# Two attention blocks on one core: scaled fp16 parts in place of f32r parts, and the row sum scaled on ScalarE

## The chip, the cores and the metric

One of the eight cores of a Trainium2 chip runs the kernel. The metric is the device time of one execution in microseconds. Before the change the median of 3 runs is 421.03 us (420.3 to 421.5).

## The reference

`x` is 4 images of 256 channels by 1024 positions, float32. Two blocks follow each other:

```python
# block 0, for each image
h = group_norm(x)                                  # 32 groups of 8 channels
q, k, v = wq@h + bq, wk@h + bk, wv@h + bv
w = softmax(q.T @ k / 16)                          # 1024 x 1024
x = x + wo @ (v @ w.T) + bo
# block 1, on the result
att_c = softmax(rowmax(x@x.T) - x@x.T)             # 256 x 256, over channels
fb, fc, fd = wb@x + bb, wc@x + bc, wd@x + bd       # 32, 32 and 256 channels
att_s = softmax(fb.T @ fc)                         # 1024 x 1024
out = (beta * att_c@x + x) + (alpha * fd@att_s.T + x)
```

## The kernel before, in words

**Precision by parts.** A product of two float32 operands is made of three matmuls: high by high, high by low and low by high (`product`, lines 872 to 875, where L873, L874 and L875 are the three in order). In block 1 and in all attention sums the parts are fp16. In block 0 the normalised input (`xn_h`, `xn_l`), the folded weights A = wq^T wk (`a_w`) and B = (wo wv)^T (`b_w`) and the projected rows (`g_h`, `g_l`) are float32r parts. The scores of block 1 come from `fb_parts` and `fc_parts`, also float32r, which hold all three products stacked in 96 rows, so that one matmul (L997) does the work of three.

**Steps.** For each image b of block 0: statistics (`bn`, `MEAN`, `spread`, `VAR`, `gvar`, `rstd`, `st1`), normalisation (`xn`, `xnh`, `xnl`; in halves `x0n`, `x0h`, `x0l` for image 0), two projections `G.b.c` (12 matmuls of 512 columns), two `V.b.u` (24 of 256 columns), eight score tiles `S0.b.j` of 128 rows (12 matmuls of 512 columns) and two sums `O0.b.c`. For each image of block 1: `FBC`, `FD`, the channel attention (`ATT`, `AT`, `ET`), eight score tiles `S2.b.j` (2 matmuls of 512 columns) and two sums `O2.b.c`.

**A score tile's way** (64 of them): TensorE fills a PSUM slot (three slots, `SLOTS`, each of two banks, handed round among all steps in PE order); VectorE takes the negative row maximum (`max`, L690) and, for S2 only, scales it (L694); ScalarE takes the exponential with the row sum (`exp`, L422, which gives an ACTIVATE and an ACTIVATION_READ_ACCUMULATOR); VectorE scales the row sum (L702) and takes its reciprocal (L704), both being step `r`; ScalarE makes the high fp16 piece (`a`, L431) and VectorE the low one (`b`, L550); a DMA transpose on SP's queue brings both to `land`; the sum `O` reads them. `exps` and `pieces` have two buffers each, so the exponential of tile n waits for the pieces of tile n-2.

**Order.** Five lists written out by hand (`PE_ORDER`, `ACT_ORDER`, `DVE_ORDER`, `POOL_ORDER`, `SP_ORDER`, lines 25 to 88) give the order of steps on every engine; each engine does them strictly in order and waits on semaphores. `Ox3` means three of a sum's steps (each 6 matmuls).

**The start.** SP's queue loads x of image 0, the group-norm vectors, wo, wv, wd and small vectors, then x of images 1 and 2; ScalarE's queue loads wk, bq and wq. TensorE multiplies the weights (`BG` for the bias, `A`, `B`, and `W` for the rest) while VectorE makes the statistics; `SV` finds bounds of the weights from which `lS` (`fixed_scales`, lines 611 to 642) makes powers of two that scale the fp16 parts. VectorE's list starts with

```python
    bn.0 gb spread.0 gvar.0 st1.0 x0n.0.0 x0n.0.1 bn.1 x0n.1.0 x0l.0.1 lA x0l.0.0 lB x0n.1.1 spread.1 hb gvar.1 cb
    lG.0.0 lS max0.0.0 st1.1 bnd.0 r0.0.0 xn.1.0 max0.0.1 max0.0.2 r0.0.1 b0.0.0 b0.0.1 max0.0.3 r0.0.2 bn.2 lV.0.1
```

`G.0.0` needs the low and high parts of A and of the first half of the input; `S0.0.0` needs `lG.0.0` and the parts of both halves.

## Time and profile before

| what | value |
|---|---|
| runs | 420.3, 421.03, 421.5 us |
| the profiled execution's own time | 419.87 us |
| its span, first to last instruction | 418.1 us |
| TensorE matmuls | 399.9 us busy, 96% of the span |
| TensorE weight loads (beside the matmuls) | 253.9 us, 61% |
| VectorE | 307.5 us, 74% |
| ScalarE | 240.4 us, 57% |
| GpSimd | 47.5 us, 11% |
| granted TensorE clock, mean | 0.998 of full speed |

Engines in the rows: PE is TensorE's matmul, PEld its weight load, DVE is VectorE, ACT ScalarE, POOL GpSimd, SP SyncE; a q behind a name is that engine's queue. L12 is line 12 of the kernel. The end of a matmul is modelled and matmuls are pipelined, so one matmul's duration (380 to 410 ns) is longer than the distance from one start to the next; what a matmul costs is read from starts. `a<-b` is output and inputs, `x` a count.

### The profile page before, as it was taken

The numbers are of one execution on the slowest core, as the hardware profiler recorded it, in microseconds if no ns is written. First come the engines' busy times: TensorE is split into PE (matmuls) and PEld (weight loads), VectorE is DVE, ScalarE is ACT, GpSimd is POOL, SyncE is SP. The second block draws the span as 40 slices with busy tenths as digits, with TensorE's granted clock in tenths as the row PEclk, the third lists the DMA queues.
The fourth block names the chain that finished last, engine by engine and source line by source line (L and its number), as shares of the span: only waits on it lengthen the run. The fifth ranks groups of instructions, "written<-read, shape, count | busy, mean of one in ns | idle before, by whom it ended". The sixth has DMA issues, their size and how long they took to land.

```text
span 418.1 us, 5612 instructions
## 1 busy us (share of the span) xinstructions
PE 399.9 (96%) x2012; PEld 253.9 (61%) x2012; DVE 307.5 (74%) x564; ACT 240.4 (57%) x314; POOL 47.5 (11%) x47
## 2 busy tenths in 40 slices
...
GB/s 229 261 45 19 119 114 96 89 68 186 17 100 122 78 88 118 101 120 157 103 88 114 51 102 125 151 102 50 163 140 57 134 88 152 104 195 124 167 192 51
DMA packets 155739, 47.89 MB, mean 115 GB/s; under 512 B 152320, under 2 KB 153664, under 8 KB 155712
## 3 DMA queue, kind: packets, MB, share of 16 engines
...
q14 instruction: 11, 0.09, 0.1%
...
## 4 chain that ended last, share of the span: by engine, by line
PE 86%; DVE 7%; SPq 2%; issue 2%; DMA 1%; ACT 1%; POOL 0%; DVEq 0%; ACTq 0%
PE sum_ps L873 14%; PE sum_ps L875 14%; PE sum_ps L874 14%; PE score_ps L873 12%; PE score_ps L875 12%; PE score_ps L874 12%; PE score_ps L997 4%; PE score_ps L1018 3%; DVE pieces L550 1%; DMA x<-in_x_dram 1%; DVE bn_raw L726 1%; PE score_ps L1027 1%; DVE x L852 1%; SPq L292 1%; SPq L278 1%
## 5 line engine op out<-in xcount | busy, mean ns | idle before, releaser
L550 DVE SCALAR_TENSOR_TENSOR pieces<-exps,recip,pieces 128x1024 f16<-128x1024 f32 x64 | 88.6, 1388 | 19.9 <-ACT pieces L431 19.5
L431 ACT ACTIVATE pieces<-exps,recip 128x1024 f16<-128x1024 f32 x64 | 72.9, 1143 | 37.6 <-DVE recip L704 27.6
L690 DVE TENSOR_REDUCE negmax<-score_ps 128x1 f32<-128x1024 f32 x64 | 77.4, 1215 | 10.8 <-PE score_ps L997 5.3
L422 ACT ACTIVATE exps<-score_ps,negmax 128x1024 f32<-128x1024 f32 x32 | 35.6, 1112 | 38.1 <-DVE negmax L690 31.7
L873 PE MATMUL score_ps<-xn_h,g_h 128*128 128x512 f32 x128 | 52.8, 412 | 1.1 <-DVE g_l L547 1.1
L422 ACT ACTIVATE exps<-score_ps,negmax_s,scales 128x1024 f32<-128x1024 f32 x32 | 38.4, 1201 | 24.2 <-DVE negmax_s L694 13.8
L875 PE MATMUL score_ps<-xn_h,g_l 128*128 128x512 f32 x128 | 50.1, 391 | 0.0
L874 PE MATMUL score_ps<-xn_l,g_h 128*128 128x512 f32 x128 | 49.9, 390 | 0.0
L873 PE MATMUL sum_ps<-land,fd_h 128*128 128x512 f16 x128 | 48.8, 381 | 0.0
L873 PE MATMUL sum_ps<-land,v_h 128*128 128x512 f16 x128 | 48.7, 381 | 0.0
L874 PE MATMUL sum_ps<-land,fd_h 128*128 128x512 f16 x128 | 48.5, 379 | 0.0
L875 PE MATMUL sum_ps<-land,fd_l 128*128 128x512 f16 x128 | 48.5, 379 | 0.0
L874 PE MATMUL sum_ps<-land,v_h 128*128 128x512 f16 x128 | 48.5, 379 | 0.0
L875 PE MATMUL sum_ps<-land,v_l 128*128 128x512 f16 x128 | 48.5, 379 | 0.0
L378 POOL TENSOR_TENSOR x_parts<-x,x_parts 128x1024 f16<-128x1024 f32 x7 | 15.9, 2272 | 138.3 <-ACT x_parts L395 138.3
L364 POOL TENSOR_TENSOR xn_l<-xn,xn_h 128x1024 fp32r<-128x1024 f32 x6 | 15.5, 2600 | 131.9 <-ACT xn_h L408 87.0
L873 PEld LDWEIGHTS score_ps<-xn_h,g_h 128*128 128x128 f32 x128 | 24.1, 188 | 7.2 <-DVE g_l L547 1.2
L875 PEld LDWEIGHTS score_ps<-xn_h,g_l 128*128 128x128 f32 x128 | 24.0, 188 | 5.3
L874 PEld LDWEIGHTS score_ps<-xn_l,g_h 128*128 128x128 f32 x128 | 24.1, 188 | 4.9
L997 PE MATMUL score_ps<-fc_parts,fb_parts 96*128 96x512 f32 x64 | 24.5, 465 | 0.0
L859 DVE SCALAR_TENSOR_TENSOR x<-sum_ps,scales,x 128x512 f32<-128x512 f32 x16 | 11.3, 745 | 17.2 <-PE sum_ps L875 17.2
L873 PEld LDWEIGHTS sum_ps<-land,fd_h 128*128 128x128 f16 x128 | 12.5, 98 | 17.7 <-issue 5.2
...
## 6 DMA issues: line engine op xcount, KB each, us to landing
...
land<-pieces SPq DMA_TRANSPOSE x64, 3.7
...
```

The lines of the kernel that those rows point to most:

```text
L364: pool.tensor_tensor(xn_l[:, m, :], xn[:, m, :], xn_h[:, m, :].bitcast(f32), ALU.subtract)\
L378: pool.tensor_tensor(x1_parts[b % 2][:, c, :, 1, :], xs[b][:, :, cols(c, QC)], x1_parts[b % 2][:, c, :, 0, :], ALU.subtract).then_inc(x1_s ...
L422: act.activation(exps[:, n % 2, :], score_ps[s][:, :], ACT.Exp, bias=bias, scale=scale, accum_out=rowsum[:, at]).then_inc(score_done[s], 1)
L431: act.activation(pieces[:, n % 2, 0, :], exps[:, n % 2, :], ACT.Copy, scale=recip[:, n % RING:n % RING + 1]).then_inc(high_piece, 1)
L550: return dve.scalar_tensor_tensor(dst, src, scale, high_part, ALU.mult, ALU.subtract)
L690: last = dve.tensor_reduce(negmax[:, at], ps[:, :], AX.X, ALU.max, negate=True)
L859: dve.scalar_tensor_tensor(part, sum_ps[m][:, :], of_batch(b, OUT_UNIT), part, ALU.mult, ALU.add).then_inc(sum_done[m], 1)
L873: pe.matmul(dst, lhs[0], rhs[0], start=start, stop=False)
L874: pe.matmul(dst, lhs[0], rhs[1], start=False, stop=False)
L875: return pe.matmul(dst, lhs[1], rhs[0], start=False, stop=stop)
L997: last = pe.matmul(ps[:, cols(n, QC)], fb_parts[0:3 * C8, cols(j)], fc_parts[0:3 * C8, cols(n, QC)], start=True, stop=True)
L1018: last = pe.matmul(ps[:, cols(m, QC)].rearrange("p (a k q) -> p a k q", a=2, k=CH), xt[:, c, m, 0, u, :], xt[:, c, :, :, u, :].rearrange(" ...
```

## The change

- The f32r tensors of block 0 and of block 1's scores become fp16, which needs scales: bounds on h (`HX`, `hs`), on the rows of wq (`wkA`, `wqA`, `rb`) and on A's product (`TG`, `gs`) give powers of two for h, A and g; B is copied from PSUM (`cB`), bounded in `SV` by two more matmuls, and cut into parts once `lS` is done (`hB`, `lB`). The group-norm bound (`hb`) goes to the head of VectorE's list.
- Every exponential now has a scale read from memory and a scaled maximum: the scores of block 0 need it too, so `max` has its second instruction for all 64 tiles.
- The row sum is scaled on ScalarE, behind the exponential and after a wait for it, in place of VectorE.
- gn_w, gn_b and bq are loaded from GpSimd's queue, ahead of its constants; wo and wv move from SP's queue to ScalarE's, behind wk and wq.
- All five orders are new. In VectorE's, `bn.1` and `x0n.1.0` move behind the low parts that `G.0.0` needs.

The core of the diff:

```diff
...
+PIECES = {"S0": 2.0 ** 15, "S2": 2.0 ** 11}
 PIECE = 2.0 ** 15
...
 PE_ORDER = """
-    BG MEAN.0 WO VAR.0 A B W MEAN.1 G.0.0 VAR.1 SV S0.0.0 S0.0.1 S0.0.2 S0.0.3 V.0.1 G.0.1 V.0.0 S0.0.4 S0.0.5
-    S0.0.6 S0.0.7 O0.0.0x3 MX.0 O0.0.0x2 G.1.0 O0.0.0x3 S0.1.0 S0.1.1 S0.1.2 O0.0.1x2 MEAN.2 S0.1.3 O0.0.1x4 VAR.2
...
+    BG MEAN.0 WO HX VAR.0 A TG W B G.0.0 MEAN.1 SV S0.0.0 S0.0.1 S0.0.2 S0.0.3 G.0.1 V.0.0 VAR.1 S0.0.4 S0.0.5 V.0.1
+    S0.0.6 S0.0.7 O0.0.0x6 MEAN.2 G.1.0 MX.0 O0.0.0x1 VAR.2 O0.0.0x1 S0.1.0 S0.1.1 S0.1.2 S0.1.3 O0.0.1x3 MX.1
+    O0.0.1x5 FBC.0.0 FD.0.0 V.1.0 FBC.0.1 V.1.1 O0.1.0x1 S2.0.0 ATT.0 S2.0.1 O0.1.0x1 AT.0 O0.1.0x2 S2.0.2 O0.1.0x1
...
 ACT_ORDER = """
...
+    hWO wkA wqA x0h.0.0 x0h.0.1 x0h.1.0 hA hW1 x0h.1.1 cB hG.0.0 hB exp0.0.0 exp0.0.1 a0.0.0 a0.0.1 exp0.0.2 hG.0.1
+    exp0.0.3 hV.0.0 a0.0.2 a0.0.3 hW2 exp0.0.4 exp0.0.5 a0.0.4 xnh.1.0 hV.0.1 xnh.1.1 a0.0.5 exp0.0.6 exp0.0.7
...
 DVE_ORDER = """
...
+    hb bn.0 gb spread.0 hs gvar.0 rb st1.0 x0n.0.0 x0n.0.1 gs hw x0l.0.0 lA x0l.0.1 bn.1 x0n.1.0 cb x0n.1.1 aB
+    spread.1 lG.0.0 lS max0.0.0 max0.0.1 r0.0.0 max0.0.2 r0.0.1 b0.0.0 lB b0.0.1 max0.0.3 lG.0.1 r0.0.2 r0.0.3
+    gvar.1 lV.0.0 st1.1 max0.0.4 b0.0.2 b0.0.3 max0.0.5 r0.0.4 bn.2 r0.0.5 lW xn.1.0 xn.1.1 b0.0.4 max0.0.7 lV.0.1
...
-        a_w = [sb(f"a_w_{p}", [P, CH, C], f32r) for p in "hl"]
-        b_w = [sb(f"b_w_{p}", [P, CH, C], f32r) for p in "hl"]
+        a_w = [sb(f"a_w_{p}", [P, CH, C], f16) for p in "hl"]
+        b_w = [sb(f"b_w_{p}", [P, CH, C], f16) for p in "hl"]
...
-        xn_h, xn_l = sb("xn_h", [P, CH, N], f32r), sb("xn_l", [P, CH, N], f32r)
-        g_h, g_l = sb("g_h", [P, CH, QC], f32r), sb("g_l", [P, CH, QC], f32r)
+        xn_h, xn_l = sb("xn_h", [P, CH, N], f16), sb("xn_l", [P, CH, N], f16)
+        g_h, g_l = sb("g_h", [P, CH, QC], f16), sb("g_l", [P, CH, QC], f16)
...
-        fb_parts, fc_parts = sb("fb_parts", [P, N], f32r), sb("fc_parts", [P, N], f32r)
...
+        fb_parts, fc_parts = sb("fb_parts", [P, N], f16), sb("fc_parts", [P, N], f16)
+        abs_w, abs_bbc = sb("abs_w", [P, 2 * CH, C], f32r), sb("abs_bbc", [P, CH, 3 * C8], f32r)
+        h_wide, ones_r = sb("h_wide", [P, CH, P], f32r), sb("ones_r", [P, P], f32r)
...
-            load_v(GN_W, gn_w, gn_loaded)
-            load_v(GN_B, gn_b, gn_loaded)
-            load_w(wo_sb, wo, wo_loaded)
-            load_w(wv_sb, wv, wv_loaded)
...
+            for n, v, loaded in ((GN_W, gn_w, gn_loaded), (GN_B, gn_b, gn_loaded), (BQ, bq, bq_loaded)):
+                with nc.allow_non_contiguous_dma(reason="vectors of 256 words"):
+                    pool.dma_start(vecs[:, n, :], v.rearrange("(m p) -> p m", p=P)).then_inc(loaded, 16)
...
-            act.dma_start(wk_sb, wk.rearrange("(m p) c -> p m c", p=P)).then_inc(wk_loaded, 16)
...
-            act.dma_start(wq_sb, wq.rearrange("(m p) c -> p m c", p=P)).then_inc(wq_loaded, 16)
+            for dst, src, loaded in ((wk_sb, wk, wk_loaded), (wq_sb, wq, wq_loaded), (wo_sb, wo, wo_loaded),
+                                     (wv_sb, wv, wv_loaded)):
+                act.dma_start(dst, src.rearrange("(m p) c -> p m c", p=P)).then_inc(loaded, 16)
...
-                if kind(use) == "S0":
-                    bias, scale = negmax[:, at], 1.0
-                else:
-                    bias, scale = negmax_s[:, at], of_batch(numbers(use)[1][0], SCORE_UNIT)
-                act.activation(exps[:, n % 2, :], score_ps[s][:, :], ACT.Exp, bias=bias, scale=scale,
+                act.activation(exps[:, n % 2, :], score_ps[s][:, :], ACT.Exp, bias=negmax_s[:, at], scale=unit_of(use),
                                accum_out=rowsum[:, at]).then_inc(score_done[s], 1)
+                act.wait_ge(score_done[s], SCORE[use][1] + 1)
+                act.activation(scaled[:, at], rowsum[:, at], ACT.Copy, scale=1.0 / PIECES[kind(use)])\
+                    .then_inc(scaled_made, 1)
...
+                if name == "wkA":
+                    act.wait_ge(wk_loaded, 16)
+                    act.activation(abs_w[:, 0:CH, :], wk_sb, ACT.Abs).then_inc(wk_abs, 1)
+                elif name == "wqA":
+                    act.wait_ge(wq_loaded, 16)
+                    for m in range(CH):
+                        last = act.activation(abs_w[:, CH + m, :], wq_sb[:, m, :], ACT.Abs,
+                                              accum_out=vecs[:, WQ_SUM, m:m + 1])
+                    last.then_inc(wq_abs, 1)
+                elif name == "hA":
                     s, ps = full("A")
...
+                    act.wait_ge(a_scale_made, 1)
+                    act.activation(a_w[0][:, :, :], rows_of(ps[:, 0:QC]), ACT.Copy,
+                                   scale=block0[:, A_SCALE:A_SCALE + 1]).then_inc(score_staged[s], 1)
+                elif name == "cB":
+                    s, ps = full("B")
+                    high(b_full[:, :, :], rows_of(ps[:, 0:QC])).then_inc(score_done[s], 1)
...
                 elif name == "hB":
-                    s, ps = full("B")
-                    high(b_w[0][:, :, :], rows_of(ps[:, 0:QC])).then_inc(score_staged[s], 1)
+                    act.wait_ge(fixed_made, 1)
+                    act.activation(b_w[0][:, :, :], b_full[:, :, :], ACT.Copy,
+                                   scale=fixed[:, B_SCALE:B_SCALE + 1]).then_inc(b_high, 1)
...
+            def h_scale():
+                s, ps = wait_full("HX")
+                dve.tensor_reduce(of0(H_MAX), ps[:, 0:P], AX.X, ALU.max).then_inc(score_done[s], 1)
+                dve.wait_ge(score_done[s], SCORE["HX"][1] + 1)
+                link(dve.tensor_scalar(of0(H_MAX), of0(H_MAX), 1.01, LEAST, ALU.mult, ALU.max))
+                power_of_two(H_MAX)
+                dve.tensor_scalar(of0(U_SCALE), of0(H_INVERSE), 2.0 ** 3, None, ALU.mult)
+                link(dve.tensor_scalar(of0(U_UNIT), of0(H_POWER), 2.0 ** -4, None, ALU.mult))
+                dve.tensor_scalar(vecs[:, U_W, :], vecs[:, GN_W, :], of0(U_SCALE), None, ALU.mult)
+                dve.tensor_scalar(vecs[:, U_B, :], vecs[:, GN_B, :], of0(U_SCALE), None, ALU.mult).then_inc(affine0_made, 1)
+                dve.wait_ge(affine0_made, 1)
+            def r_bound():
+                dve.wait_ge(bq_loaded, 16)
+                dve.wait_ge(wq_abs, 1)
+                link(magnitude(vecs[:, BQ_BOUND, :], vecs[:, BQ, :]))
+                link(dve.scalar_tensor_tensor(vecs[:, R_BOUND, :], vecs[:, WQ_SUM, :], of0(H_MAX), vecs[:, BQ_BOUND, :],
+                                              ALU.mult, ALU.add))
+                for m in range(CH):
+                    last = dve.tensor_scalar(h_wide[:, m, :], ones[:, :], vecs[:, R_BOUND, m:m + 1], None, ALU.mult)
+                last.then_inc(r_bound_made, 1)
+            def g_scales():
+                s, ps = wait_full("TG")
+                dve.tensor_reduce(of0(T_MAX), ps[:, 0:C], AX.X, ALU.max).then_inc(score_done[s], 1)
+                dve.wait_ge(score_done[s], SCORE["TG"][1] + 1)
+                link(dve.tensor_scalar(of0(T_MAX), of0(T_MAX), 1.01, LEAST, ALU.mult, ALU.max))
+                power_of_two(T_MAX)
+                _, used, _ = SCORE["BG"]
+                dve.wait_ge(score_done[SCORE["BG"][0]], used + 1)
+                dve.tensor_scalar(vecs[:, G_BIAS, :], vecs[:, K_BIAS, :], of0(T_INVERSE), 2.0 ** 13, ALU.mult, ALU.mult)
+                dve.tensor_scalar(of0(A_SCALE), of0(T_INVERSE), 2.0 ** 13, of0(U_UNIT), ALU.mult, ALU.mult)
+                dve.tensor_scalar(of0(SCORE_0), of0(T_POWER), 2.0 ** -14 * float(C) ** -0.5, of0(U_UNIT),
+                                  ALU.mult, ALU.mult).then_inc(a_scale_made, 1)
+                dve.wait_ge(a_scale_made, 1)
...
-                last = dve.tensor_reduce(negmax[:, at], ps[:, :], AX.X, ALU.max, negate=True)
-                if kind(use) == "S2":
-                    b = numbers(use)[1][0]
-                    link(last)
-                    last = dve.tensor_scalar(negmax_s[:, at], negmax[:, at], of_batch(b, SCORE_UNIT), None, ALU.mult)
-                last.then_inc(score_staged[s], 1)
+                link(dve.tensor_reduce(negmax[:, at], ps[:, :], AX.X, ALU.max, negate=True))
+                dve.tensor_scalar(negmax_s[:, at], negmax[:, at], unit_of(use), None, ALU.mult)\
+                    .then_inc(score_staged[s], 1)
...
-                s, used, _ = SCORE[use]
-                dve.wait_ge(score_done[s], used + 1)
-                dve.tensor_scalar(scaled[:, at], rowsum[:, at], 1.0 / PIECE, None, ALU.mult).then_inc(scaled_made, 1)
...
+                for m in range(CH):
+                    last = pe.matmul(ps[:, QC + C:QC + 2 * C], ones_r[:, :], abs_w[:, m, :], start=(m == 0),
+                                     stop=(m == CH - 1))
...
-                    done("B")
+                    pe.wait_ge(b_made, 1)
...
+                elif name == "HX":
+                    pe.wait_ge(h_diag_made, 1)
+                    s, ps = enter(step)
+                    pe.matmul(ps[:, 0:P], ones[:, :], x_diag[:, :], start=True, stop=True).then_inc(score_full[s], 1)
+                elif name == "TG":
+                    pe.wait_ge(wk_abs, 1)
+                    pe.wait_ge(r_bound_made, 1)
+                    s, ps = enter(step)
+                    for m in range(CH):
+                        last = pe.matmul(ps[:, 0:C], h_wide[:, m, :], abs_w[:, m, :], start=(m == 0), stop=(m == CH - 1))
+                    last.then_inc(score_full[s], 1)
...
```

## Rows read from the trace of the kernel before

**Rows 1.** The page, busy time of the engines: us (share of the span) xinstructions.
```profile
PE 399.9 (96%) x2012; PEld 253.9 (61%) x2012; DVE 307.5 (74%) x564; ACT 240.4 (57%) x314; POOL 47.5 (11%) x47
```
**Rows 2.** Busy time by stretch: us, engines' busy (xinstructions), PEclk, DMA share, GB/s.
```profile
28.60:50.00 21.40, 21.39 (x116) 18.52 (x117) 19.46 (x57) 12.97 (x18) 0.00 (x0) 1.00 0.22 50
110.00:160.00 50.00, 50.00 (x269) 32.49 (x268) 42.84 (x86) 34.40 (x45) 8.88 (x4) 1.00 0.37 85
360.00:390.00 30.00, 30.00 (x167) 16.79 (x166) 27.10 (x49) 21.57 (x32) 2.67 (x5) 1.00 0.68 159
```
**Rows 3.** TensorE's waits from 28.6 to 413.5 us: us, times, longest.
```profile
PE score_ps L873 <- DVE g_l L547: 1.1, 1, 1.1
PE score_ps L873 <- DVE fc_parts L547: 0.6, 1, 0.6
PE sum_ps L873 <- DVE x L859: 0.4, 1, 0.4
```
**Rows 4.** Timeline of TensorE: start, us (modelled), line, out<-in, shape.
```profile
113.38 0.28 PE L873 MATMUL score_ps<-d_w_h,x_parts 128*128 128x256 f16 x1
...
116.01 0.38 PE L873 MATMUL sum_ps<-land,v_h 128*128 128x512 f16 x1
...
189.53 0.38 PE L875 MATMUL score_ps<-x_parts,bbc_w_l 128*96 128x512 f16 x1
...
192.55 0.28 PE L873 MATMUL score_ps<-b_w_h,xn_h 128*128 128x256 f32 x1
...
195.42 0.63 PE L997 MATMUL score_ps<-fc_parts,fb_parts 96*128 96x512 f32 x2
...
196.99 0.38 PE L875 MATMUL sum_ps<-land,fd_l 128*128 128x512 f16 x1
...
197.68 0.39 PE L873 MATMUL sum_ps<-land,fd_h 128*128 128x512 f16 x1
...
198.77 0.38 PE L875 MATMUL sum_ps<-land,fd_l 128*128 128x512 f16 x1
...
201.74 0.39 PE L873 MATMUL sum_ps<-land,fd_h 128*128 128x512 f16 x1
...
389.25 0.38 PE L873 MATMUL sum_ps<-land,fd_h 128*128 128x512 f16 x1
...
399.39 0.38 PE L875 MATMUL sum_ps<-land,fd_l 128*128 128x512 f16 x1
```
**Rows 5.** Groups by line and shape: busy us, mean ns of one, idle before and releaser.
```profile
L422 ACT ACTIVATE exps<-score_ps,negmax_s,scales 128x1024 f32<-128x1024 f32 x32 | 38.4, 1201 | 24.2 <-DVE negmax_s L694 13.8 <-DVE pieces L550 10.2
L422 ACT ACTIVATE exps<-score_ps,negmax 128x1024 f32<-128x1024 f32 x32 | 35.6, 1112 | 38.1 <-DVE negmax L690 31.7 <-DVE pieces L550 6.4
L422 ACT ACTIVATION_READ_ACCUMULATOR exps<-score_ps,negmax 128x1 f32 x32 | 6.1, 192 | 0.0
L450 ACT ACTIVATE fc_parts<-sum_ps 128x192 fp32r<-128x192 f32 x1 | 0.3, 322 | 0.0
L702 DVE TENSOR_SCALAR scaled<-rowsum 128x1 f32<-128x1 f32 x64 | 9.4, 147 | 11.7 <-ACT exps L422 11.1
L694 DVE TENSOR_SCALAR negmax_s<-negmax,scales 128x1 f32<-128x1 f32 x32 | 6.9, 214 | 1.1
```
**Rows 6.** The start: VectorE's and TensorE's timeline, TensorE's wait, loads and GpSimd's issues.
```profile
16.95 2.47 DVE L726 BATCH_NORM_STATS2 bn_raw<-x 128x6 f32<-128x512 f32 x4 [2.04 <-DMA x<-in_x_dram]
...
28.61 0.47 PE L873 MATMUL score_ps<-xn_h,g_h 128*128 128x512 f32 x1 [1.06 <-DVE g_l L547]
...
PE score_ps L893 <- DMA vecs<-in_L_conv_bq_dram: 7.8, 1, 7.8
...
vecs<-in_L_conv_gn_b_dram SPq DMA_DIRECT2D x1, 1.0 KB, 7.9
...
L383 POOL DMA_DIRECT2D out_dram<-x x16 | 8.8, 553 | 75.9 <-DVE x L859 75.8
```

More of the change, by code:

```diff
@@ L95, in kind @@
+TWICE = {"A", "G", "V", "S0", "S2", "FBC", "FD", "ATT", "ET"}
 def kind(step):
@@ L260, in of_batch, with unit_of @@
             return scales[0:rows, b, n:n + count]
+        def unit_of(use):
+            if kind(use) == "S0":
+                return block0[:, SCORE_0:SCORE_0 + 1]
+            return of_batch(numbers(use)[1][0], SCORE_UNIT)
         def turn_of(use):
@@ L591, in magnitude, with powers @@
                 return dve.scalar_tensor_tensor(dst, src, -1.0, src, ALU.mult, ALU.max)
+            def powers(bound, up, down):
+                dve.tensor_scalar(up.bitcast(u32), bound.bitcast(u32), EXPONENT, None, ALU.bitwise_and)
+                return dve.tensor_scalar(down.bitcast(u32), bound.bitcast(u32), EXPONENT, EXPONENT,
+                                         ALU.bitwise_xor, ALU.bitwise_and)
             def h_bound():
@@ L598, in h_bound, with of0, power_of_two @@
                                               ALU.mult, ALU.add))
+                link(dve.tensor_reduce(x_bound[:, 0, 0:1], vecs[:, H_BOUND, :], AX.X, ALU.max))
                 dve.wait_ge(consts_made, 8)
-                dve.tensor_scalar(ones_r, ones[:, :], 1.0, None, ALU.mult)
+                dve.tensor_scalar(x_diag[:, :], ident[:, :], x_bound[:, 0, 0:1], None, ALU.mult).then_inc(h_diag_made, 1)
+            def of0(n):
+                return block0[:, n:n + 1]
+            def power_of_two(n):
+                link(powers(of0(n), of0(n + 1), of0(n + 2)))
@@ L601, in h_bound, with h_wide_bound @@
+            def h_wide_bound():
+                s, used, _ = SCORE["TG"]
+                dve.wait_ge(score_full[s], used + 1)
+                dve.tensor_scalar(ones_r[:, :], ones[:, :], 1.0, None, ALU.mult)
                 for m in range(CH):
@@ L603, in h_bound @@
                 last.then_inc(h_bound_made, 1)
-            def powers(bound, up, down):
-                dve.tensor_scalar(up.bitcast(u32), bound.bitcast(u32), EXPONENT, None, ALU.bitwise_and)
-                return dve.tensor_scalar(down.bitcast(u32), bound.bitcast(u32), EXPONENT, EXPONENT,
-                                         ALU.bitwise_xor, ALU.bitwise_and)
             def fixed_scales():
@@ L642, in fixed_scales @@
+                dve.tensor_scalar(of(by_unit, 3), of(ones, 0), 2.0 ** -7, None, ALU.mult).then_inc(fixed_made, 1)
                 dve.wait_ge(fixed_made, 1)
@@ L772, in _ @@
                     dve.wait_ge(xn0_high, CH * c + m + 1)
-                    low(xn_l[:, m, half], xn[:, m, half], xn_h[:, m, half].bitcast(f32)).then_inc(xn0_split[c], 1)
+                    low(xn_l[:, m, half], xn[:, m, half], xn_h[:, m, half]).then_inc(xn0_split[c], 1)
                 elif name == "xn":
```

215 lines of the change are left out of this document (107 added, 108 removed).

## The prediction

> **What bounds the kernel now.** I read the page's busy shares first, then busy time by stretch, then TensorE's waits, then its timeline start by start. VectorE is busy 74% and ScalarE 57% of the span [rows 1], so neither is the bound on average. By stretch, TensorE is busy in all of each of three stretches, 28.6 to 50, 110 to 160 and 360 to 390 us, with the granted clock at 1.00 (the upper level, 2.4 GHz) [rows 2]. From the first score tile to the last sum it waits 2.1 us altogether, three times [rows 3]. So from 28.6 us on the kernel is as long as TensorE's own list of matmuls; before 28.6 us it is a chain of small steps on all engines, and behind the last sum there is a short tail of one update and a store, which the change leaves alone. In the same three stretches VectorE is busy 91%, 86% and 90% [rows 2]: that is where it could take over if TensorE gets faster.
>
> A matmul's price is the distance between starts. In a sum, 47 distances of fp16 matmuls with 512 columns take 10.14 us, 0.2157 each; a whole FD step, 24 fp16 matmuls of 256 columns, takes 2.63 us [rows 4].
>
> **Part 1: fp16 parts on TensorE.** For each kind of f32r step I take the time from the last start before it to the first start after it, less the 0.216 us of that last fp16 matmul where there is one, and set the fp16 price against it [rows 4].
> - S0: 201.74 - 198.77 - 0.216 = 2.754 us for 12 matmuls; fp16 12 x 0.2157 = 2.588. Saves 0.166, for 32 tiles 5.3 us.
> - G: 192.55 - 189.53 - 0.216 = 2.804; fp16 2.588. Saves 0.216, 8 steps, 1.7 us.
> - V: 195.42 - 192.55 = 2.87; fp16 as FD, 2.63. Saves 0.24, 8 steps, 1.9 us.
> - S2: 197.68 - 196.99 - 0.216 = 0.474; fp16 0.431. Saves 0.043, 32 tiles, 1.4 us.
>
> Together 10.3 us. All of it but the first G lies on the path. The sizes are those of single steps; with starts given to 0.01 us the sum may be 9 to 11.5.
>
> The measured rows decide here, since a rule says otherwise: the Trainium skill, page "TensorE: Matmul & The Clock Gate", section "Back-to-back issue gap", works the distance of matmuls out from the moving columns alone, some 216 ns for 512 at the upper clock, without regard to the operand's type. By it this part would save nothing. The fp16 rows agree with its figure; the f32r rows, 0.230 us each, do not.
>
> **Part 2: the softmax chain of a tile.** VectorE loses L702, 64 x 0.147 = 9.4 us, and gains L694 for the 32 tiles of block 0, 32 x 0.214 = 6.9 us [rows 5]: 2.5 us less in all, but 0.07 us more for an S0 tile and 0.15 less for an S2 tile. ScalarE gains 64 small activations. The trace has none of 128x1; the accumulator read at 0.192 us is the nearest row, the 192-element activation at 0.322 the upper bound [rows 5]. I take 0.2, so 13 us (at most 21), and 32 exponentials with a scale from memory, 1.201 in place of 1.112, 2.8 us [rows 5]. ScalarE goes from 240 to about 256 us, 63% of the new span. No engine but TensorE is near its limit on average, so I cost this part at nothing. Its cover is that TensorE has other steps (sums, projections) between two score tiles. Without that cover the chain of one S0 tile is longer by 0.214 and a semaphore (0.25), 0.09 for the exponential and 0.05 to 0.18 for the sum's scaling behind a wait (0.1): some 0.45 us; that of an S2 tile by 0.1. The wait that ScalarE now has for its own exponential holds the next `a` or `exp` on its queue, and VectorE's reciprocal behind it: that is the 0.1.
>
> **Part 3: the start.** Between the statistics of image 0 and the first G, VectorE gets 22 more instructions (8 in `hs`, 4 in `rb`, 7 in `gs`, 3 in `hw`). None is wider than 256 elements; at 0.147 to 0.214 us each [rows 5] that is 3.2 to 4.7 us, say 4.5 with the waits for `HX` and `TG`. In return `bn.1` goes behind the first G: 2.47 us, and the 2.04 us for which VectorE stands before it waiting for x of image 1 [rows 6]: 4.5 us back. Even. But `bn.1` must then be done, with `spread.1` behind it, in front of `lG.0.0`, from where `lB` and `hb` go away: I take 1.0 us later for the first S0 tile, 28.61 to 29.6 [rows 6], with -1 to +3 as bounds. The lower end is the case in which everything of `bn.1` hides under the first G's matmuls.
>
> The three vector loads move from two queues onto GpSimd's. Today BG starts at 7.8 us because bq lands then, and gn_b takes 7.9 us [rows 6]. On GpSimd's queue three issues of 0.55 us [rows 6] come first, so that the last would land at about 10.5 us if it also took 7.9: BG, which MEAN.0 stands behind on TensorE's list, 2.7 us later. It could also be quicker, as the loads no longer stand behind x. wo and wv, which gate `WO` and `B`, now stand behind wk and wq alone instead of behind x, and GpSimd's constants come 1.7 us later. Better than -1 it can't be: `A` needs wq, which is no sooner. These bounds are inside the -1 to +3.
>
> **Part 4: the new orders.** With a list shorter by 10 us and the same other engines, more steps of TensorE will find something late. The cover is VectorE's idle 26% [rows 1]. Today such waits sum to 2.1 us [rows 3]; I take 3.1, 1.0 us more. The lower end is 2 us less (none left), the upper 5 us more: in the three dense stretches, 101 of the 385 us, no saving at all (10.3 x 101/385 = 2.7) and 2.3 for the longer chain of five S0 tiles there. What would be late next is `lFBC` and `lG`, as today, and the low pieces `b` before the sums.
>
> **Sum.** Against the profiled execution's own 419.87 us: -10.3 + 0 + 1.0 + 1.0 = -8.3, that is 411.6. The median of the runs lies 1.16 us above that execution, so 412.7 us for the median, 2.0% faster. A measurement of this kernel can tell some 0.3% (1.3 us) from no change.
>
> **Rivals.**
> 1. *VectorE and ScalarE give back part.* The dense stretches of rows 2 and others like them become bound by the softmax chain. For it: 86 to 91% there, and the ScalarE exponentials that already wait for VectorE's maximum 31.7 us [rows 5]. Against it: TensorE has waited 2.1 us in 385 so far. Half of the saving gone and 1.5 us of start: 421.0 - 5.1 + 1.5 = 417.4, up to 419.5. Chance 0.19.
> 2. *The fp16 parts are no faster.* Then only the start and the new chain remain: 421.0 + 1.0, 421 to 422. This is what the skill's rule above would make of it. For it: nothing in this trace. Against it: the same 12 matmuls 0.166 us apart in rows 4. A partial saving balanced by waits ends at the same place. Chance of the two together 0.08.
> 3. *Slower: the softmax chain is the bound in most of the kernel.* Place: `max`, `exp`, `scaled`, `r`, `a`, `b` of one tile after the other. Price: a pair of tiles (one S0, one S2) is longer by 0.55 us where the chain ends last; where TensorE does, the pair saves 10.3/32 = 0.32. It decides from the point where the chain ends last for over 0.32/(0.32 + 0.55) = 37% of the 32 pairs, 12 of them. With half of them: 421.0 + 16 x 0.55 - 16 x 0.32 + 1.0 = 425.7. For it: the dense stretches, and two buffers only for exponentials and pieces. Against it: VectorE's total falls by 2.5 us, and at 64 tiles in some 375 us there are 5.9 us for a tile, against about 3 us of VectorE's work on it. Chance 0.08.
>
> A fourth, on the good side: the start comes out earlier by 1 us and the waits vanish, 412.7 - 2 - 3 = 407.7. Chance 0.07.
>
> **How the numbers follow.** My forecast of 409 to 416 us has 0.58, rival 1 0.19, rival 2 0.08, rival 3 0.08, the good case 0.07. Faster by over 0.3% are the forecast, rival 1 and the good case: 0.84; the same 0.08; slower 0.08. The range takes in the good case and rival 1: 407 to 419. What it leaves out is rivals 2 and 3 and the far ends, under 0.2.
>
> **What would show it.** In the changed kernel: a row of S0 matmuls with starts 0.216 us apart; V steps of 2.63 us; S2 pairs of 0.43. The first S0 tile at 28 to 31 us. ScalarE with 64 activations of 128x1 near 0.2 us and some 256 us busy; VectorE near 305. TensorE's waits after that tile at 2 to 5 us, and the tail as long as today. The prediction is wrong if S0's distance stays near 0.23 (rival 2), if TensorE waits over 8 us for VectorE or ScalarE (rivals 1 and 3), or if the first S0 tile comes after 32 us.

## The result and the profile after

The changed kernel takes **414.73 us** in the median of 4 runs (414.07 to 415.63); the kernel before took 421.26 beside it (420.3 to 421.66). The ratio is 0.985, 95% interval 0.9821 to 0.9878. The forecast was 412.7 in a range of 407 to 419. The profiled execution took 414.23 us, its span is 412.5.

The page, busy time of the engines, and below it the granted clock in 40 slices; it answers to [rows 1]:

```profile
PE 391.2 (95%) x2018; PEld 204.4 (50%) x2018; DVE 303.0 (73%) x556; ACT 257.6 (62%) x384; POOL 49.1 (12%) x50
...
PEclk9998999999999999999999999999999999999998
```

TensorE lost 8.7 us of busy time, VectorE 4.5, and ScalarE gained 17.2. The 8 in the fourth slice is new; the one in the last slice lies behind the last matmul. The same three stretches as in [rows 2] (length, PE, PEld, DVE, ACT, POOL, then PEclk):

```profile
28.60:50.00 21.40, 19.54 (x95) 9.71 (x96) 16.98 (x51) 12.09 (x20) 0.86 (x2) 0.92 0.27 50
110.00:160.00 50.00, 49.92 (x250) 24.26 (x248) 43.52 (x75) 39.33 (x60) 7.34 (x3) 1.00 0.53 93
360.00:390.00 30.00, 30.00 (x156) 15.26 (x155) 24.04 (x38) 20.21 (x35) 2.70 (x5) 1.00 0.76 150
```

From 110 us on TensorE is as full as before, with VectorE at 87% and 80%. The first stretch is the one that became worse: TensorE works later, and the clock's mean is 0.92. TensorE's waits from 30.45 us to the end, beside [rows 3]:

```profile
PE score_ps L954 <- DVE g_l L569: 2.4, 1, 2.4
PE sum_ps L954 <- DMA land<-pieces: 1.1, 1, 1.1
PE sum_ps L954 <- DVE x L940: 0.4, 1, 0.4
```

The first of them lies in front of the first score tile. TensorE's timeline around that tile, then two steps from the middle, S0 at 132.79 and V at 100.76 (each with the first start behind it), and one S2 pair; it answers to [rows 4, 6]:

```profile
30.45 0.38 PE L954 MATMUL score_ps<-xn_h,g_h 128*128 128x512 f16 x1 [2.39 <-DVE g_l L569]
...
31.10 0.38 PE L954 MATMUL score_ps<-xn_h,g_h 128*128 128x512 f16 x1
31.31 0.59 PE L955 MATMUL score_ps<-xn_l,g_h 128*128 128x512 f16 x1
31.70 0.63 PE L956 MATMUL score_ps<-xn_h,g_l 128*128 128x512 f16 x1
32.12 0.63 PE L954 MATMUL score_ps<-xn_h,g_h 128*128 128x512 f16 x1
...
34.94 0.38 PE L955 MATMUL score_ps<-xn_l,g_h 128*128 128x512 f16 x1
...
100.76 0.27 PE L954 MATMUL score_ps<-b_w_h,xn_h 128*128 128x256 f16 x1
103.38 0.38 PE L954 MATMUL score_ps<-x_parts,bbc_w_h 128*96 128x512 f16 x1
...
108.59 0.60 PE L1081 MATMUL score_ps<-fc_parts,fb_parts 96*128 96x512 f16 x2
109.02 3.62 PE L1102 MATMUL score_ps<-xt 128*128 128x512 f16 x16
...
132.79 0.38 PE L954 MATMUL score_ps<-xn_h,g_h 128*128 128x512 f16 x1
135.38 0.27 PE L954 MATMUL score_ps<-d_w_h,x_parts 128*128 128x256 f16 x1
```

An S0 step takes 2.59 us, a V step 2.62, an S2 pair 0.43: the prices of Part 1. But from 31.31 to 34.94 us nine distances take 3.63 us where 9 x 0.2157 = 1.94 were due, so 1.7 us are lost. The windows say why (same columns as above):

```profile
30.00:31.00 1.00, 0.55 (x3) 0.32 (x4) 1.00 (x4) 0.00 (x0) 0.00 (x0) 1.00 0.00 0
31.00:32.00 1.00, 1.00 (x5) 0.35 (x3) 0.93 (x7) 0.00 (x0) 0.00 (x0) 0.67 0.00 0
32.00:33.00 1.00, 1.00 (x4) 0.32 (x3) 0.93 (x10) 0.00 (x0) 0.00 (x0) 0.50 0.00 0
33.00:34.00 1.00, 1.00 (x4) 0.42 (x3) 0.93 (x12) 0.00 (x0) 0.00 (x0) 0.50 0.06 16
34.00:35.00 1.00, 1.00 (x5) 0.34 (x3) 0.00 (x1) 0.72 (x1) 0.00 (x0) 0.62 0.00 0
35.00:36.00 1.00, 1.00 (x6) 0.43 (x5) 1.00 (x1) 0.00 (x0) 0.00 (x0) 1.00 0.00 0
```

The granted clock falls to 0.50, the level of 1.2 GHz, and comes back to 2.4 GHz at about 35 us. Just before, TensorE had waited 1.5 us for SV's operand and, after a microsecond of work, 2.4 us for `g_l`. VectorE's timeline shows who made it wait:

```profile
9.02 0.23 DVE L613 SCALAR_TENSOR_TENSOR x_bound<-vecs 128x2 f32<-128x2 f32 x2 [9.02 <-DMA vecs<-in_L_conv_gn_b_dram]
...
9.88 2.47 DVE L800 BATCH_NORM_STATS2 bn_raw<-x 128x6 f32<-128x512 f32 x4
...
13.43 0.17 DVE L591 TENSOR_TENSOR square<-diff 128x8 f32<-128x8 f32 x1
...
26.74 0.93 DVE L589 TENSOR_TENSOR diff<-bn_raw,stat 128x8 f32<-128x8 f32 x1
27.70 1.08 DVE L591 TENSOR_TENSOR square<-diff 128x8 f32<-128x8 f32 x1
...
28.90 1.41 DVE L569 SCALAR_TENSOR_TENSOR g_l<-score_ps,vecs,g_h 128x512 f16<-128x512 f32 x2
```

and GpSimd's timeline what ran beside it:

```profile
26.11 2.65 POOL L384 TENSOR_TENSOR xn_l<-xn,xn_h 128x512 f16<-128x512 f32 x2 [9.04 <-DVE xn L609]
```

`diff` and `square` work on 8 elements and took 0.17 us each for image 0; beside GpSimd's two subtractions they take 0.93 and 1.08, and `lG.0.0` stands behind them. The first two rows are the other part of the delay: `hb` waits for gn_b until 9.02 us, and `bn.0`, which follows it on VectorE's list, starts at 9.88, though the first half of image 0 was there at 4.3 us in the kernel before.

**The sum closes.** The first score tile comes at 30.45 instead of 28.61: +1.84. From there to the start of the last matmul it is 376.95 us instead of 384.25: -7.30. The tail is 0.14 shorter. In all -5.60, which is 418.1 to 412.5. Of the -7.30, +1.7 is from the clock, +1.24 from a wait for a transpose at 60.9 us (the next start comes 1.46 after the last one, not 0.22), -0.6 from a wait of [rows 3] (`fc_parts`) that is gone; the -9.6 that are left are put down to the steps themselves.

### The profile page after: what moved, and what is told of

It is laid out like the page before. It is cut to its first block, busy times and chain, and to the rows that moved or that the text cites. A ratio compares the mean times of both kernels' runs of the same rounds, so it can differ in the third digit from the quotient of the medians.

```text
span 412.5 us, 5690 instructions
## 1 busy us (share of the span) xinstructions
PE 391.2 (95%) x2018; PEld 204.4 (50%) x2018; DVE 303.0 (73%) x556; ACT 257.6 (62%) x384; POOL 49.1 (12%) x50
## 4 chain that ended last, share of the span: by engine, by line
PE 89%; DVE 5%; DMA 3%; issue 1%; POOL 1%; SPq 0%; POOLq 0%; DVEq 0%
PE sum_ps L954 15%; PE sum_ps L955 15%; PE sum_ps L956 15%; PE score_ps L954 12%; PE score_ps L955 12%; PE score_ps L956 12%; PE score_ps L1081 3%; PE score_ps L1102 3%; DMA vecs<-in_L_conv_gn_b_dram 2%; DMA land<-pieces 2%; DVE bn_raw L800 1%; PE score_ps L1111 1%; DVE pieces L572 1%; DVE xn L609 0%; DVE x L940 0%
## 5 line engine op out<-in xcount | busy, mean ns | idle before, releaser
L430 ACT ACTIVATE exps<-score_ps,negmax_s,block 128x1024 f32<-128x1024 f32 x32 | 38.4, 1199 | 27.8 <-DVE negmax_s L771 21.7
L954 PE MATMUL score_ps<-xn_h,g_h 128*128 128x512 f16 x128 | 49.0, 383 | 2.4 <-DVE g_l L569 2.4
L956 PE MATMUL score_ps<-xn_h,g_l 128*128 128x512 f16 x128 | 49.3, 385 | 0.0
L955 PE MATMUL score_ps<-xn_l,g_h 128*128 128x512 f16 x128 | 49.2, 385 | 0.0
L778 DVE RECIPROCAL recip<-scaled 128x1 f32<-128x1 f32 x64 | 9.8, 157 | 17.3 <-ACT scaled L433 16.9
L377 POOL TENSOR_TENSOR xn_l<-xn,xn_h 128x1024 f16<-128x1024 f32 x6 | 12.8, 2131 | 80.1 <-ACT xn_h L420 80.1
L954 PEld LDWEIGHTS score_ps<-xn_h,g_h 128*128 128x128 f16 x128 | 12.6, 99 | 17.7 <-DVE g_l L569 3.0
L954 PEld LDWEIGHTS sum_ps<-land,v_h 128*128 128x128 f16 x128 | 12.6, 98 | 15.8 <-issue 2.1
L956 PEld LDWEIGHTS score_ps<-xn_h,g_l 128*128 128x128 f16 x128 | 12.6, 98 | 15.5 <-issue 0.6
L956 PEld LDWEIGHTS sum_ps<-land,v_l 128*128 128x128 f16 x128 | 12.5, 98 | 15.1
```

The source lines that it names most:

```text
L377: pool.tensor_tensor(xn_l[:, m, :], xn[:, m, :], xn_h[:, m, :], ALU.subtract)\
L430: act.activation(exps[:, n % 2, :], score_ps[s][:, :], ACT.Exp, bias=negmax_s[:, at], scale=unit_of(use), accum_out=rowsum[:, at]).then_in ...
L954: pe.matmul(dst, lhs[0], rhs[0], start=start, stop=False)
L955: pe.matmul(dst, lhs[0], rhs[1], start=False, stop=False)
L956: return pe.matmul(dst, lhs[1], rhs[0], start=False, stop=stop)
```

## The experiments

All are edits of the changed kernel. The table gives, for each, the median, the ratio to the kernel before, and from the profiled execution the start of the first S0 matmul, the time from there to the start of the last matmul, whether the clock falls behind the first score tile in that execution, and the longest wait for a landing transpose.

| kernel | median us | ratio (95%) | first S0 | S0 to last | fall | landing wait |
|---|---|---|---|---|---|---|
| before | 421.26 | | 28.61 | 384.25 | no | none |
| after | 414.73 | 0.9821-0.9878 | 30.45 | 376.95 | yes | 1.1 |
| e1_block0_f32r | 422.29 | 0.9992-1.0038 | 30.61 | 383.71 | yes | none |
| e2_sum_on_vector | 415.46 | 0.9824-0.9885 | 30.49 | 376.94 | yes | 1.3 |
| e9_four_scalings | 415.08 | 0.9832-0.9912 | 30.40 | 377.73 | yes | 1.0 |
| e5_busy_start | 411.90 | 0.9732-0.9793 | 30.62 | 374.33 | no | none |
| e10_busy_before_sv | 412.44 | 0.9754-0.9828 | 30.41 | 376.08 | yes | none |
| e11_busy_behind_sv | 411.71 | 0.9741-0.9808 | 30.70 | 374.69 | no | none |
| e3_loads_first | 414.50 | 0.979-0.985 | 29.65 | 377.05 | yes | 1.1 |
| e4_spread_late | 411.79 | 0.9732-0.9791 | 29.25 | 375.70 | no | 1.2 |
| e6_norm_early | 411.71 | 0.9748-0.9805 | 28.07 | 375.84 | no | 1.2 |
| e8_start_anew | 411.52 | 0.9738-0.9801 | 27.67 | 374.70 | no | none |
| e12_start_short | 408.62 | 0.9677-0.9738 | 26.80 | 374.57 | no | 0.5 |

**Is the gain the fp16 parts?** (e1) `a_w`, `b_w`, `xn_h`, `xn_l`, `g_h` and `g_l` become float32r again, as in the line shown, and the parts of S2 stay fp16:

```diff
-xn_h, xn_l = sb("xn_h", [P, CH, N], f16), sb("xn_l", [P, CH, N], f16)
+xn_h, xn_l = sb("xn_h", [P, CH, N], f32r), sb("xn_l", [P, CH, N], f32r)
...
```

> Edit: the changed kernel with the 4-byte parts of before in image 0's and all later block-0 work (weights A and B, the normalised image, g), orders and scales as changed; the parts of S2 stay fp16, since all of them in 4 bytes would not fit the memory. Theory A (the gain is the shorter distance of fp16 matmuls, as in Part 1 of the prediction: S0 5.3, G 1.7, V 1.9 us): 414.7 + 8.9 = 423.6 us, 422.5 to 425, S0 starts 0.229 apart again, S2 tiles 0.43. Rival B (the operand's type does not set the distance, the gain is from the new orders): 414 to 416 us, S0 starts 0.216 apart.

It takes 422.29 us, 7.6 more, and is no longer faster than the kernel before. Its steps cost what they cost before the change: this S0 step starts at 179.97, the next step at 182.71, 2.74 us (timeline of TensorE).

```profile
179.97 0.39 PE L954 MATMUL score_ps<-xn_h,g_h 128*128 128x512 f32 x1
...
182.71 0.39 PE L954 MATMUL sum_ps<-x_parts,et_h 128*128 128x512 f16 x1
```

From the first score tile to the last matmul it is 6.76 us longer, and 8.0 if the landing wait, which this kernel lacks, is left out of the other. Theory A holds, a little short of its 8.7 (8.9 less the first G, which lies ahead of that tile) and with a median just under its range. Rival B is out: the new orders and the new chain, with S2's parts in fp16, gain nothing that can be told from no change. What makes a float32r matmul dearer is not shown: its weight load is longer too (188 ns on the page of the kernel before, 98 or 99 on that of the changed one), and no run separates the two.

**Does the softmax chain cost anything?** (e2, e9) One run takes ScalarE's scaling of the row sum back to VectorE, the other makes ScalarE do it four times.

```diff
-act.wait_ge(score_done[s], SCORE[use][1] + 1)
-act.activation(scaled[:, at], rowsum[:, at], ACT.Copy, scale=1.0 / PIECES[kind(use)]).then_inc(scaled_made, 1)
...
+dve.tensor_scalar(scaled[:, at], rowsum[:, at], 1.0 / PIECES[kind(use)], None, ALU.mult).then_inc(scaled_made, 1)
 dve.reciprocal(recip[:, at], scaled[:, at]).then_inc(recip_made, 1)
```

> Edit: the scaling of the row sum goes back from ScalarE to VectorE, in front of the reciprocal; everything else is the changed kernel. Theory I (Part 2 of the prediction costed the softmax chain at nothing, since TensorE has other steps between two score tiles): 64 small activations, 13 us, leave ScalarE and 64 small operations, about 9.4 us, come to VectorE, and the time stays at 414.0 to 415.5 us. Rival J (rival 1 of the prediction: VectorE or ScalarE gives back part of the saving): with VectorE 9 us fuller TensorE waits longer for it, 416 us or more; or, if ScalarE is the one that gives back, 413.5 or less.

```diff
+for i in range(3):
+    act.activation(spare[:, 3 * n + i:3 * n + i + 1], rowsum[:, at], ACT.Copy, scale=1.0 / PIECES[kind(use)])
 act.activation(scaled[:, at], rowsum[:, at], ACT.Copy, scale=1.0 / PIECES[kind(use)])
```

> Edit: ScalarE scales each row sum four times, three of them into a spare place, so that the chain of each tile is 0.6 us longer and ScalarE has 192 more activations, some 39 us, about 296 us in all. It measures the cover that Part 2 counted on. Theory I: the cover holds almost everywhere, the time rises by at most 2 us, 414.5 to 416.7. Rival J (rivals 1 and 3 of the prediction: the chain ends last in a good part of the kernel): 64 x 0.6 = 38 us of more chain, of which a quarter or more lands on the path, 424 us or more.

415.46 and 415.08 us, against 414.73: both inside the spread of the runs. With the scaling on VectorE the time from the first score tile to the last matmul is the same to 0.01 us (376.94); with three more activations for each tile it is 0.8 longer. The rows of ScalarE in the second (groups by line: busy, mean ns, idle before):

```profile
L435 ACT ACTIVATE spare<-rowsum 128x1 f32<-128x1 f32 x192 | 24.9, 192 | 2.0
L436 ACT ACTIVATE scaled<-rowsum 128x1 f32<-128x1 f32 x64 | 11.9, 187 | 0.0
```

The four overlap, so the chain of a tile is longer by about 24.9/64 = 0.4 us rather than the 0.6 expected. 25 us of chain in all cost at most 0.8 us of time. Theory I holds and rival J falls: Part 2 was rightly costed at nothing, and where the sum is scaled makes no difference that these runs can tell.

**What makes the clock fall?** (e5, e10, e11) Matmuls whose result nobody reads fill the waits around SV: 6 in front and 10 behind (e5, the diff shown), or only the 6 (e10) or only the 10 (e11).

```diff
 elif name == "SV":
+    idle_work(6)
     weight_bounds(step)
+    idle_work(10)
```

> Edit: 6 fp16 matmuls of 512 columns in front of SV and 10 behind it, into a free half of a score buffer; nobody reads their result. They fill the two times in which TensorE waits before the first score tile (1.47 and 2.39 us) and nothing else. Theory G (the fall of the granted clock to 0.50 at 31.3 to 34.7 us follows from that idle time): the clock stays at 1.00, starts of the first score tile are 0.216 apart throughout, and the time falls by 1.7 us to 413.0, 412.3 to 413.7. Rival H (the fall has another cause): it is still there, at about the same distance behind the first score tile, and the time is 414 to 415.5.

> Edit: of the 16 idle-filling matmuls of the run with a busy start only the 6 in front of SV; the wait of 2.4 us behind SV stays. Theory G1 (the wait next to the first score tile is what the clock follows): the fall is still there, 414 to 415.5 us. Theory G2 (the two waits together make it, either one filled is enough): no fall, S0 starts 0.216 apart, 412.3 to 413.5 us.

> Edit: only the 10 matmuls behind SV; the wait of 1.5 us in front of SV stays. Theory G1 and theory G2 both expect no fall, 411.5 to 413.5 us. Theory G3 (any idle time of 1.5 us so early brings it): the fall is still there, perhaps earlier, 414 us or more.

Without either wait the clock stays at 1.00 and the time is 411.90 us, 2.8 less than 414.73 and under the expected range: 1.7 are from the clock, and the landing wait is gone too, which was not expected. With the first wait alone filled the fall is there in the profiled execution, with the second alone filled it is not. The windows of the run with 6 in front (columns as above):

```profile
29.00:30.00 1.00, 0.00 (x0) 0.00 (x0) 1.00 (x2) 0.00 (x0) 0.00 (x0) 1.00 0.00 0
30.00:31.00 1.00, 0.59 (x2) 0.27 (x3) 1.00 (x4) 0.00 (x0) 0.00 (x0) 0.81 0.00 0
31.00:32.00 1.00, 1.00 (x4) 0.41 (x3) 0.90 (x7) 0.00 (x0) 0.00 (x0) 0.50 0.08 16
```

and of the run with 10 behind:

```profile
29.00:30.00 1.00, 1.00 (x6) 0.49 (x5) 0.97 (x4) 0.00 (x0) 0.01 (x1) 1.00 0.00 0
30.00:31.00 1.00, 0.77 (x5) 0.21 (x3) 1.00 (x2) 0.00 (x0) 0.00 (x0) 1.00 0.00 0
31.00:32.00 1.00, 1.00 (x7) 0.41 (x6) 0.96 (x6) 0.00 (x0) 0.00 (x0) 1.00 0.07 16
```

So it is the 2.4 us of idle time just in front of the first score tile that matters (theory G1), and the 1.5 us in front of SV do not bring the fall by themselves: G3 is out. In every profile of this study with that wait of 2.4 to 2.6 us (five kernels beside the changed one) the clock falls, and in none of the seven without it, the kernel before among them. G2, by which filling either wait is enough, is contradicted by the profile of the run with 6 in front, but not by its median: 412.44 us lies in the range of G2 and under that of G1. Its profiled execution is 0.9 us shorter than the changed kernel's and lacks the landing wait; and its four executions fall in two pairs, 413.3 us at a mean granted clock of 0.993 and 411.5 at 0.997 or 0.998. Only one of the first pair has a trace. That the fall stayed away in the second pair, so that the first wait has a share in it, is likely, but not shown.

The executions without a trace have a mean granted clock on record. The 3.4 us at half speed take 0.004 off that mean. The kernels that keep both waits (the changed one, e1, e2, e3 and e9) have 0.988 to 0.996 in 30 executions, the runs with the second wait filled and the one with only `spread.1` moved (e5, e11, e4) 0.996 to 1.000 in 16, which fits G1. But e6, e8 and e12, which lack the wait as well, have 0.992 to 1.000 in 18. And the kernel before, with 0.998 in its profiled execution, has 0.986 to 0.998 in 39 others, and its time goes with it:

| mean granted clock | executions of the kernel before | us |
|---|---|---|
| 0.997, 0.998 | 4 | 418.8 to 419.7 |
| 0.994 to 0.996 | 11 | 419.8 to 420.6 |
| 0.989, 0.990 | 15 | 421.2 to 422.3 |
| 0.986, 0.987 | 9 | 422.3 to 424.2 |

The lower two groups lack 0.010 and more, and the 5.2 us behind the last matmul could take off 0.006 at half speed. So the clock very likely falls among the matmuls in most executions of the kernel before as well, at places that no trace shows, and its profile shows one of its best. A "no" in the table of runs is a statement on one execution.

The Trainium skill, page "TensorE: Matmul & The Clock Gate", section "HAM oscillation — how this bites in real kernels", says that idle time between bursts of matmuls lets the clock fall and that the next burst then starts at half rate. These traces agree for a wait of 2.4 us, but for one thing: the first 0.2 to 0.9 us behind it still run at 1.00, and the 0.43 us distances follow.

**Why does the first score tile come late?** (e3, e4, e6, e8, e12) First the loads, on SyncE's queue in front of image 0 and taken off GpSimd's:

```diff
+load_v(GN_W, gn_w, gn_loaded)
+load_v(GN_B, gn_b, gn_loaded)
+load_v(BQ, bq, bq_loaded)
...
```

> Edit: the loads of gn_w, gn_b and bq are issued first on SyncE's queue, in front of image 0, and not on GpSimd's. Theory C (the first score tile is late because bq lands at 10.3 and gn_b at 9.0 us): they land before 6 us, the statistics of image 0 start when it lands (4.3 before, perhaps 1 us later now), the first score tile comes 1.5 to 3 us earlier, at 27.5 to 29 us, and the time is 412 to 413.2. Rival D (the weights or image 1 set it): the loads land earlier but the first score tile stays at 30 to 30.6 us, 414 to 415.5. Third: image 0 lands so much later behind 768 words one by one that nothing is won.

Neither theory quite: gn_b is there at 5.3 us instead of 9.0 and bq at 6.5 instead of 10.3, but image 0, whose first half was there at 4.3 us before the change, now comes at 8.5 and 10.2 (VectorE's timeline):

```profile
8.50 1.29 DVE L800 BATCH_NORM_STATS2 bn_raw<-x 128x6 f32<-128x512 f32 x2 [2.23 <-DMA x<-in_x_dram]
10.26 1.29 DVE L800 BATCH_NORM_STATS2 bn_raw<-x 128x6 f32<-128x512 f32 x2 [0.47 <-DMA x<-in_x_dram]
```

The first score tile gains 0.8 us, the clock falls as before, and the time is the same within the spread. That is the third case of the expectation for the most part.

Then VectorE's order alone, the two steps at the end of the start changed round:

```diff
-    spread.1 lG.0.0 lS
+    lG.0.0 spread.1 lS
```

> Edit: on VectorE lG.0.0 goes in front of spread.1. In the changed kernel diff and square of spread.1 take 0.93 and 1.08 us instead of 0.17 each, beside GpSimd's two subtractions of the same time. Theory E (VectorE and GpSimd hold each other up, and spread.1 is on the path): lG.0.0 starts at 26.6 instead of 28.9, the first score tile comes at 28.8 (when GpSimd's second subtraction ends) to 29.5, 0.9 to 1.7 us earlier: 413 to 413.8 us; if the idle time before it also causes the fall of the granted clock, that fall is smaller or gone: 411.3 to 412.5. Rival F: lG.0.0 now takes the hold-up itself and ends no earlier, 414 to 415.5.

It takes 411.79 us. Theory E holds, with the fall of the clock gone from the profile as well. VectorE's timeline:

```profile
26.87 1.41 DVE L569 SCALAR_TENSOR_TENSOR g_l<-score_ps,vecs,g_h 128x512 f16<-128x512 f32 x2
...
28.38 0.63 DVE L589 TENSOR_TENSOR diff<-bn_raw,stat 128x8 f32<-128x8 f32 x1
29.05 0.17 DVE L591 TENSOR_TENSOR square<-diff 128x8 f32<-128x8 f32 x1
```

and GpSimd's:

```profile
26.34 2.65 POOL L384 TENSOR_TENSOR xn_l<-xn,xn_h 128x512 f16<-128x512 f32 x2 [9.04 <-DVE xn L609]
```

`lG.0.0`, which reads PSUM and one SBUF tensor, takes the same 1.41 us beside GpSimd. `diff`, which reads two SBUF tensors, ends at 29.0 with GpSimd's work (26.34 + 2.65 = 28.99), and `square` behind it takes 0.17 again.

More of the same, with the normalised half and aB in front of `bn.1`:

```diff
-    x0l.0.1 bn.1 x0n.1.0 cb x0n.1.1 aB
-    spread.1 lG.0.0 lS
+    x0l.0.1 x0n.1.0 x0n.1.1 aB bn.1 cb
+    lG.0.0 spread.1 lS
```

> Edit, on VectorE alone: the second half of the normalised image 0 and aB go in front of bn.1, and lG.0.0 in front of spread.1. Theory E carried on: GpSimd's two subtractions start at about 23 us and are over before spread.1, SV no longer waits for aB, and the first score tile waits for lG.0.0 alone, which starts when bn.1 ends at about 26.6: first score tile at 27.8 to 28.6 us, no fall of the clock, 409.6 to 411.2 us. Rival K: bn.1 beside GpSimd's subtractions takes longer than 2.5 us, and the first score tile comes no earlier than with lG.0.0 ahead alone (29.25), 411.2 to 412.5 us.

The first score tile comes at 28.07 us as expected, 1.2 earlier than in the run before, and the clock does not fall; the profiled execution is 1.1 us shorter in span (409.0 against 410.1). The median, 411.71, is a little over the expected range and cannot be told from the last one.

The same order on VectorE from `x0l.0.1` on, and a start in a new order: gn_w, gn_b and bq on SyncE's queue behind image 0, the magnitudes of wk and wq first on ScalarE, and the lists of TensorE and VectorE so:

```diff
-PE: BG MEAN.0 WO HX VAR.0 A TG W B G.0.0
+PE: MEAN.0 HX VAR.0 BG A TG WO W B G.0.0
-DVE: hb bn.0 gb spread.0 hs gvar.0 rb
+DVE: bn.0 spread.0 hb hs gvar.0 gb rb
```

> Edit: the same order on VectorE; and gn_w, gn_b and bq on SyncE's queue behind image 0, as before the change; MEAN.0, HX and VAR.0 in front of BG on TensorE, WO behind TG; bn.0 and spread.0 in front of hb on VectorE; the magnitudes of wk and wq and the first normalised half in front of hWO on ScalarE. Theory C carried on (the start is long because the statistics of image 0 stand behind bq and gn_b, which land at 9 to 10.3 us, though the image has landed by then): the statistics run from 4.3 us on, gn_b at about 8 us is the next bound, and the first score tile comes 2 to 5 us earlier than in the kernel with the order on VectorE alone, at 23 to 26.5 us: 405.5 to 409.5 us. Rival D (the weights set it): wk, wq or wo land no earlier and A is where it was, at 14.5 us: the first score tile is within 1 us of that other kernel's.

A miss: the statistics of image 0 do run from 4.4 us, but the first score tile comes at 27.67, only 0.4 us earlier than in the run before (rival D in size, though its cause is another). A starts at 13.0 us, and on TensorE's list WO, W and B then fill the time to G.0.0 at 21.7. The next run takes that order up; its diff is against this one (on ScalarE `hWO` follows `wqA`, `cB` stands in front of `x0h.1.1` and `hW1` right in front of `hG.0.0`; on VectorE `gb` moves in front of `hs`).

```diff
-PE: MEAN.0 HX VAR.0 BG A TG WO W B G.0.0
+PE: MEAN.0 WO BG HX VAR.0 A TG B W G.0.0
-DVE: gs hw x0l.0.0 lA x0l.0.1 x0n.1.0
+DVE: gs x0l.0.0 lA x0l.0.1 hw x0n.1.0
```

> Edit: the start of the kernel with the new start again, with WO and BG in the time in which TensorE waits for gn_b, B in front of W, G.0.0 behind both, and hw on VectorE behind the low pieces of the first half. In the kernel with the new start the image and the weights have landed by 8.7 us, and A is at 13.0 us behind BG, and WO, W and B stand between TG and G.0.0. Theory C2 (what is left is TensorE's order, not the loads): HX about 1 us later, A at about 12.2, TG 15.4, G.0.0 at 19.5 to 20 instead of 21.7, the first score tile at 25 to 26.5 us instead of 27.7, no fall of the clock: 407.5 to 410.5 us, 1 to 2.5 us under the kernel with the new start. Rival L (bn.1 in front of lG.0.0 keeps the first score tile where it is): 27 to 28 us, 410.5 to 412.5 us.

**408.62 us**, ratio 0.9707 (0.9677 to 0.9738): the best of the study, 6.1 us under the changed kernel. G.0.0 starts at 21.16, not at 19.5 to 20, and the first score tile comes at 26.80, a little outside what theory C2 expected: `bn.1` in front of `lG.0.0` holds it up, so rival L has a share. The timeline of TensorE shows what is left ahead of it:

```profile
24.94 0.39 PE L962 MATMUL score_ps<-bn_raw,group_mean 128*128 128x8 f32 x2 [1.03 <-DVE bn_raw L800]
...
26.80 0.38 PE L954 MATMUL score_ps<-xn_h,g_h 128*128 128x512 f16 x1 [0.44 <-DVE g_l L569]
```

## Why the prediction was right, and where it missed

The forecast, that TensorE's list gets shorter by 10.3 us and little comes back, was the one that came true; the time is 2.0 us over it. By its own steps:

- **What bounds the kernel** held. TensorE is busy 95% of the span after the change, and from the first score tile on it waits once for more than 0.4 us.
- **Part 1** (-10.3): -9.6 is what the accounting above leaves for it from the first score tile on, where 10.1 were forecast (10.3 less the first G, which is not on the path). The run with 4-byte parts in block 0 gives the same from the other side: 8.0 for S0, G and V where 8.7 were forecast. The single steps are as forecast (2.59, 2.62, 0.43). The rule of the Trainium skill that the prediction set against the rows (page "TensorE: Matmul & The Clock Gate", section "Back-to-back issue gap"), by which the type would not matter, does not hold for the f32r parts here: that run refutes it, and rival 2 with it. S2's share of 1.4 us rests on the single steps alone (0.474 before, 0.43 after); no run put its parts back.
- **Part 2** (0): right, shown by the two runs on the chain. The estimate of 0.2 us for the small activation was measured at 203 ns, and its wait on ScalarE's own exponential, put at 0.1 us, leaves 2.0 us of idle time in 64 (groups by line):

```profile
L433 ACT ACTIVATE scaled<-rowsum 128x1 f32<-128x1 f32 x64 | 13.0, 203 | 2.0
```

- **Part 3** (+1.0): +1.84. Bq was forecast at about 10.5 us and came at 10.33. The first G at 22.53 instead of 22.20 says that the 22 new instructions and the moved `bn.1` do nearly cancel, as worked out. What was too small is the step "`bn.1` must then be done, with `spread.1` behind it, in front of `lG.0.0`", put at 1.0 us: from the first G to `lG.0.0` it is 6.37 us instead of 4.86 (22.53 to 28.90, 22.20 to 27.06), 1.5 more. `bn.1` and `x0n.1.0` bring 2.8 into that stretch, `lB`, `hb` and `gvar.1` take 1.9 out of it, and `spread.1`, which stood in it before as well, takes 0.6 more (2.35 instead of 1.79). Its hold-up beside GpSimd could be seen in the trace of the kernel before, where `diff` of image 1 took 1.28 us beside one subtraction (VectorE's timeline, and GpSimd's in the last row):

```profile
23.91 1.28 DVE L567 TENSOR_TENSOR diff<-bn_raw,stat 128x8 f32<-128x8 f32 x1
25.22 0.17 DVE L569 TENSOR_TENSOR square<-diff 128x8 f32<-128x8 f32 x1
...
27.06 1.40 DVE L547 SCALAR_TENSOR_TENSOR g_l<-score_ps,vecs,g_h 128x512 fp32r<-128x512 f32 x2
...
23.88 1.28 POOL L371 TENSOR_TENSOR xn_l<-xn,xn_h 128x512 fp32r<-128x512 f32 x1 [2.29 <-DVE xn L587]
```

- **Part 4** (+1.0): +0.6, from one new wait of 1.24 for a landing transpose and one old wait of 0.6 that went. The forecast had expected `lFBC`, `lG` or the pieces to be late.
- **Missed altogether:** the prices of Part 1 were taken at a granted clock of 1.00 for the whole kernel. A longer wait in front of the first score tile was priced as that wait alone; in the profiled execution it costs another 1.7 us at 1.2 GHz behind it.
- **The median** was put 1.16 above the profiled execution, as before the change; it is 0.50 above. The 1.16 was not a fixed distance: the profile of before is of an execution at 0.998, and most others of that kernel have a lower clock. So the 1.7 of the clock is a loss between the two profiles, and between the medians it is likely less. By the profiles, 412.7, +0.7 for Part 1, +0.84, -0.4, +1.7, -0.66 and -0.2 for the tail make 414.7. That misses of both signs cancel in part is luck.

Rival 1 (417.4 us) expected part of the saving to be given back, and part was, but not by the softmax chain of VectorE and ScalarE, which has room, as the two runs on it show. The same runs speak against rival 3.

**Left open.** The landing wait at 60.9 us: it is there in seven of the twelve kernels with the change (1.0 to 1.3 us, 0.5 in the last) and missing in five with the same work around it. In the changed kernel one of the first transposes lands 6.3 us after its issue, the median is 4.8; what it met was not tried. Also open: where the clock falls in the executions without a trace, and what share the wait in front of SV has.
